# Recommender tower on one core: products reordered among the gram units, small steps moved between engines, four features of the last tile fetched by SyncE

## The chip, the cores and the metric

The kernel runs on one core of a Trainium2 chip. The core has five engines that run side by side: TensorE (PE, with its weight loads shown apart as PEld), VectorE (DVE), ScalarE (ACT), GpSimd (POOL) and SyncE (SP). They wait for one another through semaphores. The metric is device time in microseconds; smaller is better.

## The reference

A batch of 2048 rows has 27 ids each. Every id picks a row of 128 numbers from its own table. All products of two of the 27 picked rows (351 pairs) are formed, and a first layer works on the picked rows, the pairs and 16 further numbers.

```
e = stack([tbl_f[ids[:, f]] for f in range(27)], axis=1)          # 2048 x 27 x 128
inter = einsum('bfd,bgd->bfg', e, e)[:, TRIU_I, TRIU_J]           # 2048 x 351
h = concatenate([e.reshape(2048, -1), inter, dense_ctx], axis=1)  # 2048 x 3823
h = maximum(h @ W_top1 + b_top1, 0)                               # 512
h = maximum(h @ W_top2 + b_top2, 0)                               # 256
y = h @ W_top3                                                    # 2048 x 1
```

## The kernel before

The batch is cut into 16 tiles of 128 rows. Features stand in seven groups: six of four, and one of three (group 6).

GpSimd fetches a feature of a tile with one indirect DMA (L242), 128 rows into `emb`, which has a single buffer: the gathers of a group for the next tile wait until TensorE has transposed that group of this one (`s_pe_t`). TensorE transposes each feature (L269) into `ps_t`, two banks used in turn. ScalarE rounds the transposed group into the high part of `emb_x` (L534), and VectorE subtracts to get the low part (L645, counted by `s_emb_lo`). Then the group's products with the first layer's weights can run: three matmuls for each feature (L298, L299, L300, the function `multiply`), which sum into `ps_acc`.

The pair products of a tile come from 16 gram units (`gram_unit`, two matmuls each, L323) into three PSUM banks used in turn. Even units are copied out by ScalarE (L582), odd ones by VectorE (L666), four copies each (`take_blocks`); a unit waits until the bank of three units earlier is empty. Between units stand products of the same tile, as the list `BEFORE_UNIT` says: 2 ahead of unit 0, 2 of unit 3, and 1 each of units 6, 9 and 12. After units 8 and 14 the first two groups of the next tile are transposed. Behind the last unit come layer 2 of the tile before (L400) and the products not yet done, two of them in tiles 1 to 14.

In the next tile VectorE turns the copied blocks (`turn_blocks`, one stream transpose, L680), adds the two parts (L687), copies the 16 context numbers (L698) and packs the 351 pairs (L702) into `cols`. TensorE transposes `cols` (`turn_columns`, L352), ScalarE copies them out (L550, L551), and TensorE adds their products (`multiply_columns`, L356) to the tile's sum. ScalarE applies the relu (L565), TensorE transposes h1 (`turn_h1`, L393), ScalarE copies it (L571), layer 2 follows behind the gram units, and VectorE does layer 3 (L714, L717) one tile later still. The transposed columns, the transposed h1 and the result of layer 2 share one PSUM bank, `ps_late`.

The order on each engine is written out by hand. On VectorE a tile runs: split group 0, turn blocks, split 1, add parts, context, half of the pairs, split 2, the other pairs, layer 3, splits 3 to 6, then the takes of units 1, 3 to 15. The last tile has an order of its own: gram units in pairs over more banks, a separate last feature, and the pairs divided between VectorE and GpSimd. SyncE loads weights and constants at the start and then only waits to store the output.

Of the kernel before, what the change touches and what calls it, by code (L numbers as in the profile page):

```python
# [5 lines left out]
def dlrm_tower_kernel(nc, dense_ctx, ids, tables, w_top1, b_top1, w_top2, b_top2, w_top3, out):  # L6
# [6 lines left out]
    P = 128  # L13
# [35 lines left out]
    PAIRS = UNITS // 2  # L49

    POOL_FROM = 16
    HALF = H1 // 2

    ctx = ExitStack()
    with ctx:
# [15 lines left out]

        emb_x = sb("emb_x", [P, 2, P, Q], fp32r)
        emb = sb("emb", [P, NF * D])
        g_buf = sb("g_buf", [P, 2 * Q * XW])
        gram = sb("gram", [P, NF, NF])
        cols = sb("cols", [P, NCOL])
# [30 lines left out]
        s_w_late = sem("s_w_late")  # L107
        s_gather = [sem(f"s_gather{g}") for g in range(NG)]
        s_gather_last = sem("s_gather_last")
        s_zero = sem("s_zero")  # L110
        s_ident = sem("s_ident")
        s_pads = sem("s_pads")
# [11 lines left out]
        s_sum = sem("s_sum")  # L124
        s_sum_pool = sem("s_sum_pool")
        s_cols = sem("s_cols")
        s_cols_pool = sem("s_cols_pool")
        s_cols_t = sem("s_cols_t")
        s_cols_out = sem("s_cols_out")
# [6 lines left out]
        s_h2 = sem("s_h2")  # L136
        s_y = sem("s_y")
        s_stored = sem("s_stored")

        def emb_part(part, f):  # L140
            return emb_x[:, part, :, f]
# [39 lines left out]
        @block.sync  # L181
        def _(sp):
            def load_weights(c):
                s = c % STAGES
                if c >= STAGES:
                    sp.wait_ge(s_w_lo, c - STAGES + 1)
                sp.dma_start(stage[:, s, :], w_top1[c * P:(c + 1) * P, :]).then_inc(s_w_raw[s], 16)

            sp.dma_start(idx_first[:, :], ids.rearrange("(p t) f -> p t f", t=TILES)[:, 0, :]
                         ).then_inc(s_ids_first, 16)
            sp.wait_ge(s_ids_first, 16)
            for c in range(NF):
# [13 lines left out]
            sp.dma_start(w_2[:, :, :], w_top2.rearrange("(k p) n -> p k n", p=P)  # L208
                         ).then_inc(s_w_late, 16)

            rows = dense_ctx.rearrange("(q j t) c -> j q (t c)", j=NJ, t=TILES)
            for j in range(NJ):
                sp.dma_start(ctx_rows[j * Q:(j + 1) * Q, :, :].rearrange("p t c -> p (t c)"),
                             rows[j, :, :]).then_inc(s_ctx, 16)
            sp.dma_start(b2_rows[:, :], b_top2.partition_broadcast(P)).then_inc(s_const, 16)
            sp.dma_start(w3_rows[:, :],
                         w_top3.rearrange("k o -> (k o)").partition_broadcast(P)
                         ).then_inc(s_const, 16)
            sp.wait_ge(s_y, TILES)
            sp.dma_start(out.rearrange("(p t) o -> p (t o)", t=TILES),  # L220
                         y[:, :]).then_inc(s_stored, 16)
            sp.wait_ge(s_stored, 16)

        @block.gpsimd
        def _(pool):
# [5 lines left out]
            for t in range(TILES):  # L231
                if t == 1:
                    pool.wait_ge(s_ids, 16)
                for g in range(NG):
                    if t > 0:
                        pool.wait_ge(s_pe_t, NG * (t - 1) + g + 1)
                    for f in GROUPS[g]:
                        landed = s_gather[g]
# [23 lines left out]
        def _(pe):  # L262
            def turn_group(t, g):
                n = NG * t + g
                pe.wait_ge(s_gather[g], (t + 1) * 16 * len(GROUPS[g]))
                if n >= 2:
                    pe.wait_ge(s_emb_lo, n - 1)
                for i, f in enumerate(GROUPS[g]):
                    last = pe.transpose(turned_bank(n, g)[:, :, i], emb[:, f * D:(f + 1) * D],  # L269
                                        ident[:, :])  # L270
                last.then_inc(s_pe_t, 1)

            def turn_last_group(t):

                g, n = NG - 1, NG * t + NG - 1
                pe.wait_ge(s_gather[g], 16 * ((t + 1) * len(GROUPS[g]) - 1))
                pe.wait_ge(s_emb_lo, n - 1)
                for i, f in enumerate(GROUPS[g][:-1]):
                    last = pe.transpose(turned_bank(n, g)[:, :, i], emb[:, f * D:(f + 1) * D],
                                        ident[:, :])  # L280
                last.then_inc(s_pe_t, 1)

# [75 lines left out]

            def turn_columns(t):
                pe.wait_ge(s_cols, t + 1)  # L360
                if t > 0:
                    pe.wait_ge(s_h2, t)
                if t == 0:
                    pe.wait_ge(s_ones, 2)
                for n in range(NCC):
# [74 lines left out]

            BEFORE_UNIT = [2, 0, 0, 2, 0, 0, 1, 0, 0, 1, 0, 0, 1, 0, 0, 0]
            assert len(BEFORE_UNIT) == UNITS and sum(BEFORE_UNIT) <= NF - 4 * GF

            pe.wait_ge(s_ident, 1)
# [2 lines left out]
            for t in range(TILES - 1):  # L449
# [5 lines left out]
                if t > 0:  # L455
                    turn_columns(t - 1)
                turn_group(t, 4)
                if t > 0:
                    multiply_columns(t - 1)
                multiply_group(t, 3)  # L460
                turn_group(t, 5)
                if t > 0:
                    turn_h1(t - 1)
                f = 4 * GF
                for _ in range(GF if t == 0 else 2):
                    multiply(t, f)
                    f += 1
                turn_group(t, 6)
                for k in range(UNITS):
                    for _ in range(min(BEFORE_UNIT[k], NF - f)):  # L470
# [51 lines left out]
        def _(act):  # L522
# [14 lines left out]
            def split_last_group(t):  # L537
# [5 lines left out]
                act.activation(emb_part(0, NF - 1), last_feature_bank(),  # L543
                               ACT.Copy).then_inc(s_emb_hi, 1)

            def take_columns(t):
                act.wait_ge(s_cols_t, t + 1)
                if t > 0:
# [57 lines left out]
            for t in range(TILES - 1):  # L606
                for g in range(NG):
                    if t == 0:
                        for c in GROUPS[g]:
                            split_weights(c)  # L610
                    split_group(t, g)
                    if t > 0 and g == 3:
                        take_columns(t - 1)
                    if t > 0 and g == 4:
                        relu_h1(t - 1)
                    if t > 0 and g == 5:
                        take_h1(t - 1)
                for k in range(0, UNITS, 2):
                    take_blocks(t, k)
            t = TILES - 1  # L620
            for g in range(5):
                split_group(t, g)
            take_columns(t - 1)
            relu_h1(t - 1)
            split_group(t, 5)
# [9 lines left out]
        def _(dve):  # L635
# [54 lines left out]
            def pack_pairs(t, f_from, f_to):  # L690
                if f_from == 0:
                    dve.wait_ge(s_sum, t + 1)
                    if t == 0:
                        dve.wait_ge(s_ctx, 16 * NJ)
                    else:
                        dve.wait_ge(s_cols_t, t)
                    if t < TILES - 1:
                        dve.tensor_copy(cols[:, NPAIR:NPAIR + NCTX], ctx_rows[:, t, :])  # L698
                for f in range(f_from, f_to):

                    c = f * (NF - 1) - f * (f - 1) // 2
# [6 lines left out]
            def layer_3(t):  # L708
                if t == 0:
# [1 line left out]
                dve.wait_ge(s_l2, t + 1)  # L711

                result = ps_acc[:, t % 2, 0:H2] if t == TILES - 2 else ps_late[:, 0:H2]
                dve.tensor_tensor(h2[:, :], result, b2_rows[:, :],  # L714
                                  ALU.add).then_inc(s_h2, 1)
                dve.wait_ge(s_h2, t + 1)
                dve.scalar_tensor_tensor(out=h2[:, :], in0=h2[:, :], scalar=0.0,  # L717
                                         in1=w3_rows[:, :], op0=ALU.max, op1=ALU.mult,
                                         accum_out=y[:, t:t + 1]).then_inc(s_y, 1)

# [14 lines left out]
            for t in range(TILES - 1):  # L735
                for g in range(NG):
                    if t == 0:
                        for c in GROUPS[g]:
                            split_weights(c)
                    split_group(t, g)  # L740
                    if t > 0:
                        if g == 0:
                            turn_blocks(t - 1)
# [3 lines left out]
                        if g == 2:  # L747
                            pack_pairs(t - 1, 10, NF - 1)
                            if t > 1:
                                layer_3(t - 2)  # L750
                for k in range(1, UNITS, 2):
                    take_blocks(t, k)
            t = TILES - 1
            split_group(t, 0)
            split_group(t, 1)
            turn_blocks(t - 1)
            split_group(t, 2)
# [41 lines left out]
```

## Time and profile before

| | |
|---|---|
| median of 3 runs | 578.25 us (576.67 to 578.84) |
| profiled execution | span 708.0 us; the page gives no other time for it |
| TensorE busy (matmuls / weight loads) | 574.9 us (81%) / 504.6 us (71%) |
| GpSimd busy | 416.2 us (59%) |
| VectorE / ScalarE busy | 347.6 us (49%) / 232.3 us (33%) |
| mean granted TensorE clock | 0.908 of full speed |
| moved by DMA | 37.84 MB, 53 GB/s over the span |

Busy times come from the profiled execution, which took 130 us longer than the timed ones. A share of the span is a mean over stages; what sets the end has to be read from the waits and from the order of work in a tile.

### The profile page before, as it was taken

To read this page: it belongs to the slowest core of one execution; us is meant where nothing else is said; L and a number is where in the kernel's file an instruction comes from. 1 tells how busy PE (TensorE), PEld (TensorE's weight loads), DVE (VectorE), ACT (ScalarE), POOL (GpSimd) and SP (SyncE) were. 2 spreads that over 40 slices of the span, in tenths; PEclk is the share of its full clock that TensorE was granted. 3 is DMA by queue.
4 is the path that set the end of the run, shared out by engine and by line. 5 is a ranking of instruction groups with operands and counts; after the bars stand their busy time and mean duration, and the time that the engine had idled before them with its cause. 6 is when DMAs were issued, how large, how long until landed. Compare 5 with 4: busy or idle time off the path is not lost.

```text
span 708.0 us, 7882 instructions
## 1 busy us (share of the span) xinstructions
PE 574.9 (81%) x2578; PEld 504.6 (71%) x2578; DVE 347.6 (49%) x1140; ACT 232.3 (33%) x703; POOL 416.2 (59%) x450
## 2 busy tenths in 40 slices
PE   2606688989889898959959896897968979698898
PEld 1505577868778787948848795786857868697786
DVE  4305462819264563808337281554707355372755
ACT  4204423324251513315232331514315161323441
POOL 6775565666666565665746667365664666556001
PEclk9956899989989998989989899799987999989999
DMA  6613411111111111111111111011110111111000
GB/s 211 217 52 110 131 45 44 46 46 44 45 45 50 41 49 41 48 45 39 47 29 50 44 42 52 27 49 42 46 52 26 49 41 49 42 41 46 12 1 1
DMA packets 19581, 37.84 MB, mean 53 GB/s; under 512 B 7780, under 2 KB 8804, under 8 KB 19540
## 3 DMA queue, kind: packets, MB, share of 16 engines
q0 software_dynamic: 13824, 28.34, 15.1%
q1 hardware_dynamic: 5716, 8.99, 4.0%
q8 instruction: 21, 0.34, 0.2%
q14 instruction: 20, 0.16, 0.1%
HBM read 37.30 MB, written 0.01 MB: 53 GB/s over the span
## 4 chain that ended last, share of the span: by engine, by line
PE 59%; another core or an unknown queue 20%; DVE 8%; issue 6%; ACT 5%; DMA 1%; SPq 0%; ACTq 0%; DVEq 0%
PE ps_acc L298 12%; PE ps_acc L299 11%; PE ps_acc L300 11%; PE ps_gram L323 10%; DVE g_buf L666 6%; PE ps_acc L356 6%; PE ps_t L269 5%; PE ps_gram L400 3%; ACT g_buf L582 2%; DVE emb_x L645 1%; DMA g_buf<-in_W_top 1%; ACT emb_x L534 1%; ACT h_t L571 1%; PE ps_gram L352 1%
## 5 line engine op out<-in xcount | busy, mean ns | idle before, releaser
L242 POOL DMA_INDIRECT emb<-in_tbl,idx x405 | 385.8, 953 | 233.4 <-issue 109.4
L298 PE MATMUL ps_acc<-w_hi,emb_x 128*128 128x512 f32 x432 | 211.1, 489 | 28.7 <-DVE emb_x L645 26.6
L645 DVE TENSOR_TENSOR emb_x<-ps_t,emb_x 128x512 fp32r<-128x512 f32 (+1 forms) x111 | 73.9, 667 | 249.6 <-ACT emb_x L534 165.2
L299 PE MATMUL ps_acc<-w_lo,emb_x 128*128 128x512 f32 x432 | 182.7, 423 | 0.0
L300 PE MATMUL ps_acc<-w_hi,emb_x 128*128 128x512 f32 x432 | 181.0, 419 | 0.0
L666 DVE COPY g_buf<-ps_gram 32x112 f32<-32x112 f32 x480 | 129.8, 270 | 93.6 <-PE ps_gram L323 63.1
L323 PE MATMUL ps_gram<-emb_x 128*128 128x224 f32 x480 | 99.5, 335 | 79.2 <-DVE emb_x L645 41.2
L298 PEld LDWEIGHTS ps_acc<-w_hi,emb_x 128*128 128x128 f32 x432 | 131.9, 305 | 35.3 <-DVE emb_x L645 28.0
L323 PEld LDWEIGHTS ps_gram<-emb_x 128*128 128x128 f32 x480 | 83.4, 231 | 102.0 <-DVE emb_x L645 45.1
L582 ACT ACTIVATE g_buf<-ps_gram 32x112 f32<-32x112 f32 x480 | 122.2, 255 | 99.0 <-PE ps_gram L323 64.8
L534 ACT ACTIVATE emb_x<-ps_t 128x512 fp32r<-128x512 f32 (+1 forms) x111 | 63.1, 583 | 272.7 <-PE ps_t L269 137.4
L299 PEld LDWEIGHTS ps_acc<-w_lo,emb_x 128*128 128x128 f32 x432 | 134.4, 311 | 3.9
L300 PEld LDWEIGHTS ps_acc<-w_hi,emb_x 128*128 128x128 f32 x432 | 132.6, 307 | 4.2
L269 PE MATMUL ps_t<-ident,emb 128*128 128x128 f32 x429 | 68.7, 284 | 17.5 <-DMA emb<-in_tbl,idx_first 17.1
L269 PEld LDWEIGHTS ps_t<-ident,emb 128*128 128x128 f32 x429 | 53.8, 146 | 24.6 <-issue 13.2
L680 DVE STREAM_TRANSPOSE g_buf<-g_buf 128x1792 f32<-128x1792 f32 x16 | 59.2, 3697 | 0.1
L356 PE MATMUL ps_acc<-w_cols,cols_t 128*128 128x512 f32 (+1 forms) x96 | 45.5, 609 | 4.7 <-issue 3.8
L702 DVE TENSOR_TENSOR cols<-gram,g_buf 128x26 f32<-128x26 f32 (+25 forms) x406 | 39.0, 174 | 0.0
L356 PEld LDWEIGHTS ps_acc<-w_cols,cols_t 128*128 128x128 f32 (+1 forms) x96 | 17.0, 190 | 23.3 <-issue 20.8
L242 POOL DMA_INDIRECT emb<-in_tbl,idx_first x27 | 26.9, 996 | 9.2 <-issue 7.9
L400 PE MATMUL ps_gram<-w,h_t 128*128 128x256 f32 x112 | 27.0, 385 | 0.0
L400 PEld LDWEIGHTS ps_gram<-w,h_t 128*128 128x128 f32 x112 | 20.7, 195 | 2.3
(61 smaller groups left out, 163.2 us busy)
## 6 DMA issues: line engine op xcount, KB each, us to landing
g_buf<-in_W_top SPq DMA_DIRECT2D x27, 256.0 KB
emb<-in_tbl,idx POOLq DMA_INDIRECT x405
w_cols<-in_W_top SPq DMA_DIRECT2D x1, 512.0 KB
w<-in_W_top SPq DMA_DIRECT2D x1, 512.0 KB
emb<-in_tbl,idx_first POOLq DMA_INDIRECT x27
w_cols<-in_W_top SPq DMA_DIRECT2D x1, 222.0 KB
idx<-in_ids SPq DMA_DIRECT2D x1, 216.0 KB, 4.9
ctx_rows<-in_dense_ctx SPq DMA_DIRECT2D x4, 32.0 KB
```

The costliest lines, as they stand in the source:

```text
L242: pool.indirect_dma_start(out=emb[:, f * D:(f + 1) * D], out_offset=None, in_=tables[f], in_offset=bass.IndirectOffsetOnAxis(ap=rows, axis ...
L269: last = pe.transpose(turned_bank(n, g)[:, :, i], emb[:, f * D:(f + 1) * D], ident[:, :])
L298: pe.matmul(acc, emb_part(0, f), w_hi[:, f, :], start=(f == 0), stop=False)
L299: pe.matmul(acc, emb_part(0, f), w_lo[:, f, :], start=False, stop=False)
L300: last = pe.matmul(acc, emb_part(1, f), w_hi[:, f, :], start=False, stop=False)
L323: last = pe.matmul(ps_gram[:, n % BANKS, i * NJ * XW:(i + 1) * NJ * XW], gram_weights(q), gram_stream(q), start=True, stop=True)
L356: return pe.matmul(ps_acc[:, t % 2, :], cols_t[0:k, n * P:(n + 1) * P], w_cols[0:k, n, :], start=False, stop=(n == NCC - 1))
L400: last = pe.matmul(ps_late[:, 0:H2], h1_t[:, k * P:(k + 1) * P], w_2[:, k, :], start=(k == 0), stop=(k == K2 - 1))
L534: act.activation(group_part(0, g), turned_bank(n, g), ACT.Copy).then_inc(s_emb_hi, 1)
L582: last = act.activation(target, source, ACT.Copy)
L645: dve.tensor_tensor(group_part(1, g), turned_bank(n, g), group_part(0, g).bitcast(fp32), ALU.subtract).then_inc(s_emb_lo, 1)
L666: last = dve.tensor_copy(target, source)
```

## The change

Seven edits are made together.

- TensorE: the list of products among the gram units holds two ahead of units 6 and 12 instead of one, so none is left behind layer 2 in tiles 1 to 14. The products of group 3 stand ahead of the column products instead of behind them. The transposes of h1 stand two products later.
- VectorE: the low part of group 0 of the next tile is made ahead of the take of unit 15 instead of behind it.
- ScalarE copies the context numbers instead of VectorE (except in the last tile), ahead of its split of group 2; it takes the columns ahead of its split of group 4, does the relu ahead of split 5, and takes h1 behind split 6.
- VectorE leaves the first sum of layer 3 in PSUM; the next columns wait for the end of layer 3 (`s_y`) instead of that sum (`s_h2`).
- SyncE fetches features 19 to 22 of the last tile, one row at a time: for each of 128 partitions it loads four ids into registers with one load and issues four DMAs of one table row, into a buffer of their own, `ahead`. GpSimd leaves these four gathers out. TensorE waits for all 128 rows of each.

```
-            BEFORE_UNIT = [2, 0, 0, 2, 0, 0, 1, 0, 0, 1, 0, 0, 1, 0, 0, 0]
+            BEFORE_UNIT = [2, 0, 0, 2, 0, 0, 2, 0, 0, 1, 0, 0, 2, 0, 0, 0]
...
                 turn_group(t, 4)
+                multiply_group(t, 3)
                 if t > 0:
                     multiply_columns(t - 1)
-                multiply_group(t, 3)
                 turn_group(t, 5)
-                if t > 0:
-                    turn_h1(t - 1)
                 f = 4 * GF
                 for _ in range(GF if t == 0 else 2):
                     multiply(t, f)
                     f += 1
+                if t > 0:
+                    turn_h1(t - 1)
                 turn_group(t, 6)
...
             def turn_columns(t):
                 pe.wait_ge(s_cols, t + 1)
+                pe.wait_ge(s_cols_ctx, t + 1)
                 if t > 0:
-                    pe.wait_ge(s_h2, t)
+                    pe.wait_ge(s_y, t)
...
+            sp.wait_ge(s_ids, 16)
+            for p in range(P):
+                _, picked = nc.values_load_multi_w_load_instructions(
+                    idx[p:p + 1, TILES - 1, AHEAD[0]:AHEAD[-1] + 1],
+                    engines=[mybir.EngineType.SP], min_val=0, max_val=tables[AHEAD[0]].shape[0] - 1,
+                    skip_runtime_bounds_check_because="an id is a row of its table")
+                for i, f in enumerate(AHEAD):
+                    sp.dma_start(ahead[p:p + 1, i, :], tables[f][bass.ds(picked[i], 1), :]
+                                 ).then_inc(s_ahead[i], 16)
...
                     for f in GROUPS[g]:
+                        if t == TILES - 1 and f in AHEAD:
+                            continue
...
+            def place_context(t):
+                if t == 0:
+                    act.wait_ge(s_ctx, 16 * NJ)
+                else:
+                    act.wait_ge(s_cols_t, t)
+                act.activation(cols[:, NPAIR:NPAIR + NCTX], ctx_rows[:, t, :],
+                               ACT.Copy).then_inc(s_cols_ctx, 1)
...
+                    if t > 0 and g == 2:
+                        place_context(t - 1)
+                    if t > 0 and g == 4:
+                        take_columns(t - 1)
+                    if t > 0 and g == 5:
+                        relu_h1(t - 1)
                     split_group(t, g)
-                    if t > 0 and g == 3:
-                        take_columns(t - 1)
-                    if t > 0 and g == 4:
-                        relu_h1(t - 1)
-                    if t > 0 and g == 5:
+                    if t > 0 and g == 6:
                         take_h1(t - 1)
...
-                if t < TILES - 1:
-                    dve.tensor_copy(cols[:, NPAIR:NPAIR + NCTX], ctx_rows[:, t, :])
...
-                dve.tensor_tensor(h2[:, :], result, b2_rows[:, :],
-                                  ALU.add).then_inc(s_h2, 1)
+                dve.tensor_tensor(result, result, b2_rows[:, :], ALU.add).then_inc(s_h2, 1)
...
-                    split_group(t, g)
+                    if t == 0 or g > 0:
+                        split_group(t, g)
...
                 for k in range(1, UNITS, 2):
+                    if k == UNITS - 1:
+                        split_group(t + 1, 0)
                     take_blocks(t, k)
             t = TILES - 1
-            split_group(t, 0)
             split_group(t, 1)
             turn_blocks(t - 1)
```

## Rows read from the trace of the kernel before

**Rows 1.** page, its first line and the shares of the chain by engine.

```profile
span 708.0 us, 7882 instructions
...
PE 59%; another core or an unknown queue 20%; DVE 8%; issue 6%; ACT 5%; DMA 1%; SPq 0%; ACTq 0%; DVEq 0%
```

**Rows 2.** waits, whole span: engine, line, waited for, total us, times, longest.

```profile
ACT emb_x L534 <- remote: 106.9, 16, 27.5
POOL emb L242 <- PE ps_t L269: 94.0, 35, 9.3
```

**Rows 3.** timeline of GpSimd: start us, us, engine, line, op, count [idle before, releaser].

```profile
2.78 1.14 POOL L242 DMA_INDIRECT emb<-in_tbl,idx_first  x1 [1.30 <-DMA idx_first<-in_ids]
...
36.65 0.94 POOL L242 DMA_INDIRECT emb<-in_tbl,idx_first  x1 [0.30 <-issue]
...
655.83 0.94 POOL L242 DMA_INDIRECT emb<-in_tbl,idx  x1 [0.30 <-issue]
```

**Rows 4.** timeline of TensorE, tile 2 to tile 3.

```profile
166.69 0.30 PEld L323 LDWEIGHTS ps_gram<-emb_x 128*128 128x128 f32 x2
...
166.92 1.60 PEld L400 LDWEIGHTS ps_gram<-w,h_t 128*128 128x128 f32 x8
...
168.54 0.30 PEld L298 LDWEIGHTS ps_acc<-w_hi,emb_x 128*128 128x128 f32 x1
...
169.96 0.30 PEld L298 LDWEIGHTS ps_acc<-w_hi,emb_x 128*128 128x128 f32 x1
...
172.84 0.58 PEld L269 LDWEIGHTS ps_t<-ident,emb 128*128 128x128 f32 x4
...
173.41 0.59 PE L298 MATMUL ps_acc<-w_hi,emb_x 128*128 128x512 f32 x1
...
180.99 0.30 PEld L356 LDWEIGHTS ps_acc<-w_cols,cols_t 128*128 128x128 f32 x2 [0.44 <-issue]
```

**Rows 5.** timeline of ScalarE, the same boundary.

```profile
165.52 2.13 ACT L582 ACTIVATE g_buf<-ps_gram 32x112 f32<-32x112 f32 x8 [0.21 <-issue]
...
167.67 1.08 ACT L534 ACTIVATE emb_x<-ps_t 128x512 fp32r<-128x512 f32 x2
```

**Rows 6.** timeline of VectorE, the same boundary.

```profile
162.56 5.78 DVE L666 COPY g_buf<-ps_gram 32x112 f32<-32x112 f32 x20 [1.16 <-PE ps_gram L323]
...
168.37 0.69 DVE L645 TENSOR_TENSOR emb_x<-ps_t,emb_x 128x512 fp32r<-128x512 f32 x1
...
168.98 3.71 DVE L680 STREAM_TRANSPOSE g_buf<-g_buf 128x1792 f32<-128x1792 f32 x1
...
172.60 0.66 DVE L645 TENSOR_TENSOR emb_x<-ps_t,emb_x 128x512 fp32r<-128x512 f32 x1
...
175.26 0.67 DVE L645 TENSOR_TENSOR emb_x<-ps_t,emb_x 128x512 fp32r<-128x512 f32 x1
```

**Rows 7.** timeline of TensorE, two waits among gram units of tile 6.

```profile
324.04 0.48 PE L323 MATMUL ps_gram<-emb_x 128*128 128x224 f32 x2 [0.44 <-DVE g_buf L666]
...
328.36 0.49 PE L323 MATMUL ps_gram<-emb_x 128*128 128x224 f32 x2 [0.45 <-DVE g_buf L666]
```

**Rows 8.** timeline of TensorE, tile 0 to tile 1.

```profile
90.50 0.61 PE L298 MATMUL ps_acc<-w_hi,emb_x 128*128 128x512 f32 x1 [1.94 <-issue]
...
92.59 0.63 PE L299 MATMUL ps_acc<-w_lo,emb_x 128*128 128x512 f32 x1
93.02 0.63 PE L300 MATMUL ps_acc<-w_hi,emb_x 128*128 128x512 f32 x1
```

**Rows 9.** windows: stretch, us, busy us (count) by engine, granted clock, DMA.

```profile
92.10:95.40 3.30, 3.30 (x11) 2.62 (x11) 3.28 (x3) 0.00 (x0) 0.94 (x1) 0.50 0.16 40
```

**Rows 10.** timeline of TensorE in the last tile.

```profile
663.46 1.89 PE L400 MATMUL ps_gram<-w,h_t 128*128 128x256 f32 x8
...
683.69 0.27 PE L286 MATMUL ps_t<-ident,emb 128*128 128x128 f32 x1
```

**Rows 11.** timeline of SyncE at the start.

```profile
2.52 1.75 SPq L187 DMA_DIRECT2D g_buf<-in_W_top  x4
```

More of the change, by code:

```diff
@@ L51, in dlrm_tower_kernel @@
     POOL_FROM = 16
+    AHEAD = list(range(19, 23))
+    assert (NF * (TILES - 1) + AHEAD[0]) % 4 == 0
     HALF = H1 // 2
@@ L73, in dlrm_tower_kernel @@
         emb = sb("emb", [P, NF * D])
+        ahead = sb("ahead", [P, len(AHEAD), D])
         g_buf = sb("g_buf", [P, 2 * Q * XW])
@@ L109, in dlrm_tower_kernel @@
         s_gather_last = sem("s_gather_last")
+        s_ahead = [sem(f"s_ahead{f}") for f in AHEAD]
         s_zero = sem("s_zero")
@@ L126, in dlrm_tower_kernel @@
         s_cols = sem("s_cols")
+        s_cols_ctx = sem("s_cols_ctx")
         s_cols_pool = sem("s_cols_pool")
@@ L138, in dlrm_tower_kernel, with rows_of, gathered @@
         s_stored = sem("s_stored")
+        def rows_of(t, f):
+            if t == TILES - 1 and f in AHEAD:
+                return ahead[:, f - AHEAD[0], :]
+            return emb[:, f * D:(f + 1) * D]
+        def gathered(t, g):
+            last = len([f for f in GROUPS[g] if f in AHEAD]) if t == TILES - 1 else 0
+            return 16 * ((t + 1) * len(GROUPS[g]) - last)
         def emb_part(part, f):
@@ L237, in _ @@
                     for f in GROUPS[g]:
+                        if t == TILES - 1 and f in AHEAD:
+                            continue
                         landed = s_gather[g]
@@ L264, in turn_group @@
                 n = NG * t + g
-                pe.wait_ge(s_gather[g], (t + 1) * 16 * len(GROUPS[g]))
+                pe.wait_ge(s_gather[g], gathered(t, g))
+                if t == TILES - 1:
+                    for f in GROUPS[g]:
+                        if f in AHEAD:
+                            pe.wait_ge(s_ahead[f - AHEAD[0]], 16 * P)
                 if n >= 2:
@@ L268, in turn_group @@
                 for i, f in enumerate(GROUPS[g]):
-                    last = pe.transpose(turned_bank(n, g)[:, :, i], emb[:, f * D:(f + 1) * D],
+                    last = pe.transpose(turned_bank(n, g)[:, :, i], rows_of(t, f),
                                         ident[:, :])
@@ L278, in turn_last_group @@
                 for i, f in enumerate(GROUPS[g][:-1]):
-                    last = pe.transpose(turned_bank(n, g)[:, :, i], emb[:, f * D:(f + 1) * D],
+                    last = pe.transpose(turned_bank(n, g)[:, :, i], rows_of(t, f),
                                         ident[:, :])
@@ L622, in _ @@
                 split_group(t, g)
+                if g == 1:
+                    place_context(t - 1)
             take_columns(t - 1)
@@ L692, in pack_pairs @@
                     dve.wait_ge(s_sum, t + 1)
-                    if t == 0:
-                        dve.wait_ge(s_ctx, 16 * NJ)
-                    else:
+                    if t > 0:
                         dve.wait_ge(s_cols_t, t)
-                    if t < TILES - 1:
-                        dve.tensor_copy(cols[:, NPAIR:NPAIR + NCTX], ctx_rows[:, t, :])
                 for f in range(f_from, f_to):
@@ L713, in layer_3 @@
                 result = ps_acc[:, t % 2, 0:H2] if t == TILES - 2 else ps_late[:, 0:H2]
-                dve.tensor_tensor(h2[:, :], result, b2_rows[:, :],
-                                  ALU.add).then_inc(s_h2, 1)
+                dve.tensor_tensor(result, result, b2_rows[:, :], ALU.add).then_inc(s_h2, 1)
                 dve.wait_ge(s_h2, t + 1)
-                dve.scalar_tensor_tensor(out=h2[:, :], in0=h2[:, :], scalar=0.0,
+                dve.scalar_tensor_tensor(out=h2[:, :], in0=result, scalar=0.0,
                                          in1=w3_rows[:, :], op0=ALU.max, op1=ALU.mult,
```

## The prediction

> **What bounds the kernel now.** I read the page first. Its span is 708.0 us, 130 us above the median of 578.25 us, and it puts 20% of the chain, some 141 us, down to a releaser that it can't name [rows 1]. The page gives no time for what lies around the span, so the sum below is a difference, worked out from parts of the trace in which no such wait stands, and then set on the median. The waits say where the 130 us sit: ScalarE's split of the turned features waited 106.9 us in 16 stretches for something without a name, and the gathers waited 94.0 us for TensorE's transposes [rows 2]. About one such wait falls in each tile. I take them to belong to the profiled execution alone, since 708 less 141 is 567, close to what runs without a profile need.
>
> Two things can set the pace without them. GpSimd issues one gather every 1.25 us (0.94 busy, 0.30 between) [rows 3], so 27 gathers take 33.7 us a tile and all 432 take 540 us. With the first at 2.8 us, some 3.5 us from the last issue to its turned feature (an estimate) and 24.3 us from that transpose, at 683.7 us, to the end of the span [rows 10], the gathers alone ask for about 570 us. The other is TensorE's written order. If tile 0's last feature is turned at about 40 us (its gather starts at 36.65, [rows 3]), fifteen periods and 24.3 us must fit into 578.25: a period is at most (578.25 - 40 - 24.3) / 15 = 34.3 us. So TensorE's loop and the gathers are within 0.6 us a tile of each other, and whatever lengthens TensorE's loop by more than that shows in the time.
>
> Then I read one tile boundary engine by engine, from gram unit 15 of one tile to the second group of products of the next. Unit 15's weights load at 166.69, layer 2 runs from 166.92, two left-over products from 168.54, group 0 from 169.96, its twelve matmuls 0.24 us apart, the transposes of group 2 from 172.84, and group 1 starts at 173.41 with no wait [rows 4]. ScalarE finishes its last two block takes at 167.65 and goes straight into the splits of groups 0 and 1, which take 1.08 us together [rows 5], about 0.6 for one with its end. VectorE has finished take 15 at 168.34, subtracts group 0 at 168.37, transposes the blocks from 168.98 and subtracts group 1 at 172.60, done at 173.26 [rows 6]. TensorE asks for group 1 at 173.4. That is a tie of 0.15 us, and nearly all boundaries of this kind show it.
>
> **The change, part by part.** *Split of group 0 ahead of take 15, and two products moved from behind layer 2 into the gram units.* These go together. VectorE can't begin the split before ScalarE has ended its own: 167.67 + 0.6 = 168.27 [rows 5]. Before, VectorE used that time for take 15, from about 167.2. After, it waits about 1.1 us, splits until 168.98, copies block 15 in 1.16 us (twenty copies, five takes, in 5.78), transposes until 173.8 and has group 1 ready at about 174.4 [rows 6]. TensorE no longer has 1.44 us of products (169.96 - 168.54, [rows 4]) behind layer 2. It waits some 0.5 us for group 0, starts it at 169.05, is through with it and the transposes 3.45 us later (173.41 - 169.96) at 172.5, and then waits about 2 us for group 1. From unit 15 to group 1 the way grows by 1.1 us. Everything behind it keeps its order: group 2 was ready at 175.93 [rows 6], and would be at about 176.9 against TensorE's wish at 177.9.
>
> The 1.44 us come back in the gram region. There two units of a tile waited 0.44 and 0.45 us for VectorE's copies [rows 7], with one product ahead of their triple. A second product in each place fills these waits. Bounds: if the waits are filled altogether, the region grows by 1.44 - 0.89 = 0.55 us; if the copies before them, which the added product also lets catch up, give another 0.3, by 0.25. With no filling it is 1.44. I take 0.3, nearer to the rows.
>
> *Products of group 3 ahead of the columns, first-layer transposes two products later.* The column matmuls waited 0.44 us before their first weights [rows 4]; of that some 0.2 us is the switch between forms that stays. Gain 0.2 us. Between column matmuls and the transposes of h1 stand a group of transposes and two products, 1.9 us, against a relu of 0.6, so no wait replaces it.
>
> *Context copy to ScalarE, layer 3 in PSUM.* VectorE loses a copy of 0.17 us in the stretch behind group 1, where it is now early by a microsecond again: nothing. ScalarE gets it ahead of the split of group 2, whose transposes it waits for anyway. The sum in PSUM was read from PSUM before too; I cost it at nothing between -0.05 and +0.1 us. The columns now wait for the end of layer 3 rather than its first half, 0.45 us later, with 1.6 us of room: nothing.
>
> *SyncE's 512 fetches.* They take four gathers, 5.0 us, from GpSimd's last tile. But from layer 2 at 663.46 to the last transpose at 683.69 TensorE works without a wait [rows 10], with all gathers issued by 656.8 [rows 3]. TensorE needs nearly the whole period for this tile, so if the gathers set the pace the gain is what TensorE has in hand, 0 to 0.6 us, not 5. Queued behind the fetches on SyncE is only the output. Price of a partition's turn: four issues at 0.44 us [rows 11] is 1.75 us as the lower bound; the register load and address work have no row. There is room for 128 turns of about 4 us each, from about 47 us (tile 0's transposes done, constants issued) to some 32 us before the end. I take it as hidden. The Trainium skill, DMA: Bandwidth & Descriptors, section on latency and other measured facts, gives a register load from a tensor a floor of about 600 ns; by it a turn is an estimated 2.4 us, 301 us in all, hidden as well, which no row here shows.
>
> **The sum.** Per full tile 1.1 + 0.3 - 0.2 = +1.2 us, fourteen times: +16.8 us. The last tile's boundary has its group 1 split ahead of the transpose and adds nothing but the 0.3. If the gathers held TensorE back before, part of this is absorbed: between 0 and 0.6 us a tile, I take 0.25, -3.5 us.
>
> The clock adds to it. At the boundary of tile 0, where layer 2 doesn't stand, TensorE idled for 1.94 us ahead of group 0, and the granted clock was then 0.50 (1.2 GHz of 2.4) from 92.1 to 95.4 us [rows 8, 9]. Matmuls were then 0.43 us apart rather than 0.24 [rows 4, 8], which costs 3.4 x (1 - 0.24 / 0.43) = 1.5 us. The new wait of about 2.1 us is of that kind and comes in each tile. Bounds: no fall, 0; one in every tile, 14 x 1.5 = 21 us. Of the idle stretches above 1.6 us in the trace most were followed by a fall, but many of them stand beside the nameless waits and may have been longer than recorded. I take half: +10.5 us. Together 16.8 - 3.5 + 10.5 = +23.8, which is 602.0 us on the median, and about 732 on the profiled span if the nameless waits stay as they are.
>
> **The rivals.** *The wait without the clock.* The same 1.2 us a tile, but 2.1 us of idling amid dense work leave the clock at 1.0. For it: the two levels depend on more than one idle stretch, and this one is shorter than the 3 us before most of the falls. 578.25 + 16.8 - 3.5 = 591.5 us.
>
> *Hidden behind the gathers.* TensorE's real loop is below 32.5 us, because its records are stretched by the profile; the gathers set the pace before and after, and the wait fits into the room. The last tile gives back 1 us or so. 577 to 579 us. Against it: matmuls 0.24 us apart and column matmuls at 0.43 add up to nearly 34 us with what stands between.
>
> *Faster.* VectorE's way from unit 15 to group 1 is the place. If without the profile it is 30% shorter than the recorded 7.6 us, TensorE never waits for it, and the filled 0.9 us and the column gap of 0.2 come off each tile, until the gathers stop it at 33.7 us: 15 x (34.2 - 33.7) = 7 us, 571 us. The point from which it decides is 5.4 us for that way. Against it: VectorE's parts repeat to a few hundredths of a microsecond in all tiles.
>
> *SyncE comes late.* A turn above 4.1 us makes the last tile wait at its group 4; each 0.1 us more costs 12.8 us. At 4.5 us the end is 47 + 576 + 32 = 655 us.
>
> **How the numbers follow.** Forecast with clock falls 0.44; wait without them 0.28; hidden 0.14; faster 0.10; SyncE late 0.04. A difference under 0.5%, 2.9 us, can't be told from none. Slower 0.76, same 0.14, faster 0.10. The range takes in the first three cases: from 577 (hidden) to 616 (a fall in every tile, nothing absorbed, 578 + 16.8 + 21). The forecast's own range is 594 to 616.
>
> **What would show it.** In the profile of the changed kernel: VectorE idle for about 1.1 us ahead of the split of group 0, its stream transpose 1.1 us later after unit 15; the first matmul of group 1 waiting some 2 us for VectorE, in each of fourteen tiles; no waits of gram units 8 and 14; no gap ahead of the column matmuls; the granted clock at 0.50 behind the new wait. I am wrong if group 1 starts without a wait, if SyncE's last fetch lands after the last tile's third group, or if GpSimd has no wait for TensorE's transposes left.

## The result, and the profile after

The changed kernel takes 606.8 us (605.96 to 608.17, 4 runs) against 577.94 us; the ratio is 1.0512, 95% interval 1.0492 to 1.0531. It is 28.9 us slower, where +23.8 had been forecast.

The page of the changed kernel, its span and its chain by engine; they answer to [rows 1]:

```profile
span 604.2 us, 9544 instructions
...
PE 67%; DVE 16%; ACT 6%; POOL 5%; issue 4%; DMA 1%; ACTq 0%; DVEq 0%; POOLq 0%
```

The releaser without a name is gone from the chain, and the span is 1.8 us below that execution's own time of 605.96 us. VectorE, 8% of the chain of [rows 1], now has 16%.

The waits of the changed kernel (engine, line waited for: total us, times, longest):

```profile
PE ps_acc L330 <- DVE emb_x L690: 29.5, 28, 2.1
...
POOL emb L270 <- PE ps_t L301: 12.8, 16, 2.3
```

TensorE waits 29.5 us for VectorE's low part of the split, where the trace of before has such waits at its start alone. The boundary from tile 3 to tile 4, all engines, answers to [rows 4 to 6]:

```profile
160.39 0.48 PE L355 MATMUL ps_gram<-emb_x 128*128 128x224 f32 x2 [0.25 <-ACT g_buf L623]
...
160.71 1.90 PE L433 MATMUL ps_gram<-w,h_t 128*128 128x256 f32 x8
...
161.44 1.08 ACT L567 ACTIVATE emb_x<-ps_t 128x512 fp32r<-128x512 f32 x2
162.07 0.69 DVE L690 TENSOR_TENSOR emb_x<-ps_t,emb_x 128x512 fp32r<-128x512 f32 x1 [1.44 <-ACT emb_x L567]
...
162.68 1.11 DVE L711 COPY g_buf<-ps_gram 32x112 f32<-32x112 f32 x4
...
162.91 0.58 PE L330 MATMUL ps_acc<-w_hi,emb_x 128*128 128x512 f32 x1 [0.30 <-DVE emb_x L690]
...
163.89 3.62 DVE L725 STREAM_TRANSPOSE g_buf<-g_buf 128x1792 f32<-128x1792 f32 x1
...
165.89 0.60 PE L301 MATMUL ps_t<-ident,emb 128*128 128x128 f32 x4
...
167.55 0.69 DVE L690 TENSOR_TENSOR emb_x<-ps_t,emb_x 128x512 fp32r<-128x512 f32 x1
...
168.29 0.62 PE L330 MATMUL ps_acc<-w_hi,emb_x 128*128 128x512 f32 x1 [1.81 <-DVE emb_x L690]
```

Read it from gram unit 15 (160.39) on. ScalarE splits groups 0 and 1 at 161.44. VectorE has stood idle for 1.44 us (1.1 forecast) when it subtracts group 0 at 162.07. Only then comes take 15 (162.68), then the block transpose (163.89), then group 1 (167.55 to 168.24). TensorE starts group 0 at 162.91, is through with the transposes of group 2 at about 166.5 and waits until 168.29: 1.81 us. From unit 15 to group 1 it is 7.90 us here, where [rows 4] has 173.41 less 166.69, 6.7 us.

Windows of the changed kernel at this boundary, and at the one before it, tile 2 to tile 3 (stretch, length, busy us and count by engine, granted clock, share and rate of DMA):

```profile
165.60:169.10 3.50, 1.69 (x9) 1.38 (x9) 3.44 (x3) 0.60 (x1) 2.58 (x4) 1.00 0.20 52
169.10:172.50 3.40, 3.40 (x10) 2.68 (x9) 3.37 (x29) 0.00 (x0) 2.67 (x3) 0.50 0.19 49
...
127.10:133.10 6.00, 3.95 (x18) 3.47 (x17) 5.82 (x8) 0.80 (x3) 4.64 (x5) 1.00 0.21 56
133.10:136.60 3.50, 3.50 (x17) 3.42 (x18) 3.46 (x26) 0.00 (x0) 2.72 (x3) 1.00 0.18 48
```

After the wait at 166.5 the granted clock is 0.50, the 1.2 GHz level, for 3.4 us. At the earlier boundary TensorE waited from 131.23 to 132.98, as long, and the clock stayed at 1.00. There are thirteen such waits, twelve of 1.75 to 1.81 us and one of 2.13, at the boundaries from tile 1 on; seven were followed by a fall. The tiles show the two cases apart: from unit 15 to the next tile's it is 35.32 us without a fall and 36.83 with one.

### The profile page after: what moved, and what is told of

It reads as the page before. It is cut to its first block, busy times and chain, and to the rows that moved or that the text cites. A ratio compares the mean times of both kernels' runs of the same rounds, so it can differ in the third digit from the quotient of the medians.

```text
span 604.2 us, 9544 instructions
## 1 busy us (share of the span) xinstructions
PE 545.0 (90%) x2578; PEld 484.1 (80%) x2578; DVE 347.4 (57%) x1125; ACT 232.2 (38%) x718; POOL 414.1 (69%) x446
## 4 chain that ended last, share of the span: by engine, by line
PE 67%; DVE 16%; ACT 6%; POOL 5%; issue 4%; DMA 1%; ACTq 0%; DVEq 0%; POOLq 0%
PE ps_acc L330 17%; PE ps_acc L332 14%; PE ps_acc L331 14%; DVE g_buf L725 9%; PE ps_gram L355 8%; PE ps_acc L388 7%; POOL emb L270 5%; PE ps_t L301 5%; ACT g_buf L623 4%; DVE emb_x L690 4%; DVE g_buf L711 3%; ACT emb_x L567 2%; PE ps_gram L426 1%; DMA emb<-in_tbl,idx 1%; PE ps_gram L384 1%
## 5 line engine op out<-in xcount | busy, mean ns | idle before, releaser
L330 PE MATMUL ps_acc<-w_hi,emb_x 128*128 128x512 f32 x432 | 204.3, 473 | 29.5 <-DVE emb_x L690 29.5
L332 PE MATMUL ps_acc<-w_hi,emb_x 128*128 128x512 f32 x432 | 177.5, 411 | 0.0
L331 PE MATMUL ps_acc<-w_lo,emb_x 128*128 128x512 f32 x432 | 177.3, 411 | 0.0
L301 PE MATMUL ps_t<-ident,emb 128*128 128x128 f32 x425 | 67.2, 280 | 21.6 <-DMA emb<-in_tbl,idx_first 19.8
L355 PEld LDWEIGHTS ps_gram<-emb_x 128*128 128x128 f32 x480 | 69.2, 189 | 14.0 <-ACT g_buf L623 6.8
L301 PEld LDWEIGHTS ps_t<-ident,emb 128*128 128x128 f32 x425 | 52.2, 145 | 34.7 <-issue 21.7
L355 PE MATMUL ps_gram<-emb_x 128*128 128x224 f32 x480 | 75.5, 285 | 4.7 <-ACT g_buf L623 3.5
L388 PE MATMUL ps_acc<-w_cols,cols_t 128*128 128x512 f32 (+1 forms) x96 | 44.0, 593 | 0.1
L606 ACT ACTIVATE h<-ps_acc 128x512 f32<-128x512 f32 x15 | 9.0, 598 | 72.2 <-PE ps_acc L388 72.2
L270 POOL DMA_INDIRECT emb<-in_tbl,idx_first x27 | 28.2, 1045 | 9.2 <-issue 7.6
```

Source lines behind the costliest of these rows:

```text
L270: pool.indirect_dma_start(out=emb[:, f * D:(f + 1) * D], out_offset=None, in_=tables[f], in_offset=bass.IndirectOffsetOnAxis(ap=rows, axis ...
L301: last = pe.transpose(turned_bank(n, g)[:, :, i], rows_of(t, f), ident[:, :])
L330: pe.matmul(acc, emb_part(0, f), w_hi[:, f, :], start=(f == 0), stop=False)
L331: pe.matmul(acc, emb_part(0, f), w_lo[:, f, :], start=False, stop=False)
L332: last = pe.matmul(acc, emb_part(1, f), w_hi[:, f, :], start=False, stop=False)
L355: last = pe.matmul(ps_gram[:, n % BANKS, i * NJ * XW:(i + 1) * NJ * XW], gram_weights(q), gram_stream(q), start=True, stop=True)
```

## The experiments

All times below are medians; the kernel before, run beside them, had 576.7 to 577.0 us.

**The kernel before once more.** The profile of before had 130 us more than its timed runs, and nothing in the prediction could compare tile by tile.

> The kernel before, unchanged, profiled once more. If the 130 us above the timed median, and the waits without a name, belonged to that one profiled execution, the span is now about 575 us, group 1 starts about 6.3 us after gram unit 15, and a tile takes about 34.0 us. If they belong to the kernel, the span is about 700 us again.

It ran in 577.71 us, in one run. Its span and its busy shares, then its gathers' wait for TensorE, then the boundary from tile 3 to tile 4:

```profile
span 575.9 us, 7882 instructions
## 1 busy us (share of the span) xinstructions
PE 534.1 (93%) x2578; PEld 479.4 (83%) x2578; DVE 347.4 (60%) x1140; ACT 232.1 (40%) x703; POOL 416.4 (72%) x450
```

```profile
POOL emb L242 <- PE ps_t L269: 3.4, 11, 0.3
```

```profile
157.07 0.49 PE L323 MATMUL ps_gram<-emb_x 128*128 128x224 f32 x2 [0.45 <-DVE g_buf L666]
...
157.75 0.46 PE L323 MATMUL ps_gram<-emb_x 128*128 128x224 f32 x2
...
158.67 1.08 ACT L534 ACTIVATE emb_x<-ps_t 128x512 fp32r<-128x512 f32 x2
...
159.40 0.69 DVE L645 TENSOR_TENSOR emb_x<-ps_t,emb_x 128x512 fp32r<-128x512 f32 x1
...
160.01 3.70 DVE L680 STREAM_TRANSPOSE g_buf<-g_buf 128x1792 f32<-128x1792 f32 x1
...
163.64 0.65 DVE L645 TENSOR_TENSOR emb_x<-ps_t,emb_x 128x512 fp32r<-128x512 f32 x1
...
164.44 0.59 PE L298 MATMUL ps_acc<-w_hi,emb_x 128*128 128x512 f32 x1
```

The 130 us belonged to that one profiled execution. Here the granted clock is at 1.0 in every full tile, TensorE is busy for 93% of the span, GpSimd waits 3.4 us for transposes instead of the 94.0 of [rows 2], and each of the thirteen periods from tile 1's unit 15 to tile 14's is 33.93 us. Group 1 starts at 164.44 with no wait, 0.15 us after VectorE has it ready. From the start of unit 15 to unit 15's copy, splits, block transpose and group 1, each offset is that of [rows 4 to 6] within 0.05 us: the disturbed trace had the boundary right. Cut at the same three points, a tile is (the middle of unit 15 is the end of the first of its two matmuls):

| from ... to | before | changed | difference | forecast |
|---|---|---|---|---|
| middle of unit 15 to group 1 | 6.34 | 7.53 | +1.19 | +1.1 |
| group 1 to unit 0 | 17.30 | 16.98 | -0.32 | -0.2 |
| unit 0 to middle of unit 15 | 10.30 | 10.81 | +0.51 | +0.3 |
| a tile | 33.93 | 35.32 | +1.39 | +1.2 |
| a fall of the clock, when there is one | none | +1.51 | +1.51 | +1.5 |

Thirteen periods at +1.39 and seven falls at 1.51 make 28.6 us; the spans differ by 28.3.

**Take 15 first again.** In the changed kernel:

```
                 for k in range(1, UNITS, 2):
-                    if k == UNITS - 1:
-                        split_group(t + 1, 0)
                     take_blocks(t, k)
+                    if k == UNITS - 1:
+                        split_group(t + 1, 0)
```

> The changed kernel with take 15 ahead of the split of group 0 again; the list of products stays. My theory (VectorE's way from unit 15 to group 1 holds TensorE): the split doesn't start earlier or later, since ScalarE's half ends at 1.3 us after unit 15 either way, so group 0 starts at 2.1 us as in the changed kernel, but group 1 comes 1.2 us earlier, a tile takes 34.1 us, and the clock doesn't fall since the wait shrinks from 1.8 to 0.6 us: 606.8 - 14 x 1.2 - 7 x 1.5 = 579 us. Rival (the moved products are what costs, since nothing stands behind layer 2): it stays above 595 us.

Measured 576.88 us, ratio to before 1.0002 (0.9984 to 1.0019). TensorE at the boundary from tile 3 to tile 4:

```profile
159.00 0.58 PE L330 MATMUL ps_acc<-w_hi,emb_x 128*128 128x512 f32 x1 [0.30 <-DVE emb_x L690]
...
161.98 0.60 PE L301 MATMUL ps_t<-ident,emb 128*128 128x128 f32 x4
163.02 0.62 PE L330 MATMUL ps_acc<-w_hi,emb_x 128*128 128x512 f32 x1 [0.44 <-DVE emb_x L690]
```

Group 0 starts as late as in the changed kernel, for want of ScalarE, and has the same 0.30 us of idling ahead of it. Group 1 waits 0.44 us instead of 1.81. A tile is 33.96 us, the clock falls nowhere from tile 2 to tile 14, and these two lines alone give back all 30 us. 579 had been expected.

**The wait filled.** Six matmuls of no use stand in the wait; their result is not used.

```
                 turn_group(t, 2)
+                if t > 0:
+                    pe.wait_ge(s_act_raw, UNITS // 2 * t)
+                    pe.wait_ge(s_dve_raw, UNITS // 2 * t)
+                    for _ in range(6):
+                        pe.matmul(ps_gram[:, 0, :], emb_part(0, 0), w_hi[:, 0, :],
+                                  start=True, stop=True)
                 multiply_group(t, 1)
```

> The changed kernel with six products of no use (features of group 0 into an emptied gram bank, result unused) ahead of group 1 of tiles 1 to 14, 1.44 us into a wait of 1.8. It tells the clock's share from the wait's. My theory: VectorE's way is untouched, the seven falls of the clock go, 7 x 1.5 = 10.5 us: 596 us, every tile 35.3 us. Rival (TensorE's work counts, the wait is not what bounds): the added 14 x 1.44 = 20 us show, 627 us. If falls have another cause: 607 us.

Measured 597.39 us, ratio 1.0363 (1.0326 to 1.0401). TensorE at the same boundary; the six are the middle row:

```profile
163.06 0.58 PE L330 MATMUL ps_acc<-w_hi,emb_x 128*128 128x512 f32 x1 [0.30 <-DVE emb_x L696]
...
166.40 1.74 PE L489 MATMUL ps_gram<-w_hi,emb_x 128*128 128x512 f32 x6
168.49 0.62 PE L330 MATMUL ps_acc<-w_hi,emb_x 128*128 128x512 f32 x1 [0.36 <-DVE emb_x L696]
```

84 matmuls more, and 9.4 us less. Group 1 comes 7.6 us after the middle of unit 15, as in the changed kernel, tiles take 35.3 to 35.4 us (one 35.7), and from tile 2 on no full tile has the clock below 1.0. So 20 us of the loss stay when the clock doesn't fall, and 10 are the clock behind the wait.

**The two costly edits alone, on the kernel before.**

```
-            BEFORE_UNIT = [2, 0, 0, 2, 0, 0, 1, 0, 0, 1, 0, 0, 1, 0, 0, 0]
+            BEFORE_UNIT = [2, 0, 0, 2, 0, 0, 2, 0, 0, 1, 0, 0, 2, 0, 0, 0]
...
-                    split_group(t, g)
+                    if t == 0 or g > 0:
+                        split_group(t, g)
...
                 for k in range(1, UNITS, 2):
+                    if k == UNITS - 1:
+                        split_group(t + 1, 0)
                     take_blocks(t, k)
             t = TILES - 1
-            split_group(t, 0)
```

> The kernel before with two edits alone: two products moved from behind layer 2 into the gram units, and the split of group 0 ahead of take 15. My theory: these two are the whole loss; without the gap of 0.2 us that the other edits close it is 607 + 3 = 610 us. Rival (the other edits, SyncE's fetches or the context copy carry part of the loss): below 600 us.

Measured 613.8 us, ratio 1.0635 (1.0593 to 1.0676): more than the 610 expected. A tile is 35.69 us without a fall and 37.16 with one. The 0.37 us a tile above the changed kernel are what the other edits save, nearly all of it between group 1 and unit 0 (17.33 us against 16.98); I had counted 0.2. In the profiled execution, of 617.97 us, the clock fell behind eleven of the thirteen waits instead of seven: 13 x 0.37 + 4 x 1.5 = 10.8 us, against 12.0 between the two profiled executions. Its mean granted clock was 0.956, and 0.967 to 0.972 in the other runs of this kernel, which were 3 to 5 us shorter, so the number of falls seems to vary from run to run. What decides which of these waits is followed by a fall is left open: waits of the same length, 1.75 to 1.8 us, stand on both sides.

**The early split with the old list.** The changed kernel with the list of before: two products behind layer 2.

```
-            BEFORE_UNIT = [2, 0, 0, 2, 0, 0, 2, 0, 0, 1, 0, 0, 2, 0, 0, 0]
+            BEFORE_UNIT = [2, 0, 0, 2, 0, 0, 1, 0, 0, 1, 0, 0, 1, 0, 0, 0]
```

> The changed kernel with the old list of products: two stand behind layer 2 again, and the split of group 0 stays ahead of take 15. It parts the two edits. My theory: group 1 still comes 7.53 us after unit 15, since VectorE's way sets it, but TensorE reaches it later and waits 1.1 us instead of 1.8, and the gram region is 0.5 us shorter: 34.8 us a tile, 14 x 0.5 = 7 us less than the changed kernel without falls, 589 us if the shorter wait leaves the clock alone, up to 600 us if it falls as often as before. Rival (it needs both edits for a loss): 577 us.

Measured 588.48 us, ratio 1.0190 (1.0160 to 1.0221). TensorE at the boundary from tile 3 to tile 4:

```profile
165.56 0.60 PE L301 MATMUL ps_t<-ident,emb 128*128 128x128 f32 x4
167.08 0.61 PE L330 MATMUL ps_acc<-w_hi,emb_x 128*128 128x512 f32 x1 [0.93 <-DVE emb_x L690]
```

Group 1 is at 7.5 us again, and a tile is 34.79 us. The wait is 0.93 us (1.25 in one tile), and no fall followed from tile 2 to tile 14. The early split thus puts group 1 at 7.5 us whatever the list is; the moved products cost 0.51 us of gram region and turn a wait that leaves the clock alone into one that in about half of the tiles doesn't.

**The other edits alone.** The list and the order of take 15 as before; order around the columns, context copy, layer 3 in PSUM and fetches as in the changed kernel.

> The changed kernel without its two costly edits: the old list of products among the units, take 15 ahead of the split. Left are the order around the columns, the context copy, layer 3 in PSUM and SyncE's fetches. My theory: from group 1 to unit 0 the way is 0.32 us shorter, as in the changed kernel, so a tile asks for 33.6 us against 33.93 before; the gathers ask for 33.7. Gain 14 x 0.25 = 3.5 us, 573 to 574 us. Rival (the gathers held the kernel before, and the fetches take 5 us from them): below 572 us. Rival (the fetches disturb): 577 us or more.

Measured 576.98 us over twelve runs from 573.96 to 579.98, ratio 1.0002 (0.9979 to 1.0025). The gain of 3.5 us didn't come. In the profile, whose span is 573.2 us, nine periods are 33.6 us as expected (33.96 with the moved products, in the run with take 15 first: there they eat what the columns' order saves), and the last four 34.1 to 34.65. There TensorE's transposes wait for gathers:

```profile
447.58 0.55 PE L301 MATMUL ps_t<-ident,emb 128*128 128x128 f32 x3 [0.16 <-DMA emb<-in_tbl,idx]
...
473.48 0.66 PE L301 MATMUL ps_t<-ident,emb 128*128 128x128 f32 x4 [0.42 <-DMA emb<-in_tbl,idx]
```

The four combinations of the two costly edits, the others in place, now stand side by side, as a tile's time without a fall of the clock: neither 33.59 us, the list alone 33.96 (take 15 first), the early split alone 34.79 (the old list), both 35.32. The split costs 1.20 us with the old list and 1.36 with the new; the list 0.37 without the split and 0.53 with it.

GpSimd needs 33.72 us for a tile at its steady 1.25 us a gather, but in a tile now and then a gather or two takes longer (34.1 to 34.7 us in eight of fourteen tiles here). TensorE's loop at 33.59 is below that. The timed runs scatter over 6 us, which fits gathers that are late to a varying degree; that they are the cause in the timed runs too is inferred.

**SyncE's fetches.** First the changed kernel without them: features 19 to 22 of the last tile go through GpSimd as all others.

```
-    AHEAD = list(range(19, 23))
+    AHEAD = []
...
-            for p in range(P):
-                _, picked = nc.values_load_multi_w_load_instructions(...)
-                for i, f in enumerate(AHEAD):
-                    sp.dma_start(ahead[p:p + 1, i, :], ...).then_inc(s_ahead[i], 16)
```

> The changed kernel without SyncE's fetches: GpSimd gathers all features again. My theory: with 35.3 to 36.8 us a tile against 33.7 for the gathers these are hidden, and nothing changes: 607 us, within 1. Rival (GpSimd's last tile counted): 612 us. Rival (512 small fetches had slowed something): 604 us or less.

Measured 608.04 us, ratio 1.0543 (1.0515 to 1.0572) beside the changed kernel's 1.0512: intervals that overlap, no difference shown. Its profiled execution has eight falls of the clock instead of seven, and its tiles the same 35.3 and 36.8 us. Then the fetches as the only edit on the kernel before (the loop above added, GpSimd's four gathers taken out).

> The kernel before with SyncE's fetches as its only edit. My theory: TensorE sets the pace at 33.93 us a tile, the gathers ask for 33.7, so four gathers less in the last tile give 0 to 1 us: 576 to 577 us. Rival (the gathers held the kernel before): 572 us.

Measured 576.81 us, ratio 0.9991 (0.9976 to 1.0006): nothing. SyncE in the changed kernel, all 512 fetches:

```profile
47.23 294.09 SPq L243 DMA_DIRECT2D ahead<-in_tbl  x512
```

They run from 47.2 to 341.3 us, 2.30 us for a partition's four, and are there some 230 us before the last tile's group 4 is transposed at 571.9.

**A version without the wait.** The take comes first again, and VectorE subtracts group 1 ahead of the block transpose, not behind it.

```
-                    if t == 0 or g > 0:
+                    if t == 0 or g > 1:
                         split_group(t, g)
                     if t > 0:
                         if g == 0:
+                            split_group(t, 1)
                             turn_blocks(t - 1)
...
                 for k in range(1, UNITS, 2):
+                    take_blocks(t, k)
                     if k == UNITS - 1:
                         split_group(t + 1, 0)
-                    take_blocks(t, k)
```

> The changed kernel with take 15 ahead of the split, and on VectorE the split of group 1 ahead of the block transpose, as the last tile has it. My theory: group 1 is ready 2.7 us after unit 15 and TensorE reaches it at 5.6 without a wait; a tile asks for 10.8 + 5.6 + 17.0 = 33.4 us. The gathers' 33.7 are nearly the bound: 569 us, up to 571. Rival (VectorE is then late for group 2, wanted 9.0 us after unit 15, at 8.9 to 9.0): a new wait there of 0.3 us or more, 573 us or more.

Measured 573.11 us, ratio 0.9929 (0.9911 to 0.9947): 0.7% below the kernel before, and 2 to 4 us above the 569 to 571 expected. The boundary from tile 3 to tile 4, VectorE and TensorE:

```profile
158.40 1.29 DVE L690 TENSOR_TENSOR emb_x<-ps_t,emb_x 128x512 fp32r<-128x512 f32 x2
...
159.24 0.58 PE L330 MATMUL ps_acc<-w_hi,emb_x 128*128 128x512 f32 x1 [0.30 <-DVE emb_x L690]
...
159.60 3.71 DVE L725 STREAM_TRANSPOSE g_buf<-g_buf 128x1792 f32<-128x1792 f32 x1
...
162.28 0.60 PE L301 MATMUL ps_t<-ident,emb 128*128 128x128 f32 x4
...
162.64 0.59 PE L330 MATMUL ps_acc<-w_hi,emb_x 128*128 128x512 f32 x1
```

VectorE subtracts both groups in one go at 158.40, and the transposes of group 2 run straight into group 1 (162.64). TensorE's loop falls to 33.39 us, and from tile 6 on it is held at 33.5 to 33.8: the gathers' pace. The rival's number, 573, came without its cause: from tile 2 to tile 14 TensorE never waits for group 2's low part, and the waits that are new, 0.1 to 0.2 us at a time, are for gathers. Without the fetches:

> The kernel of the run before without SyncE's fetches. Once TensorE's tile is below 33.7 us the gathers set the pace: the last one can't be issued before 541 us, which with 3.2 us to its transpose, 24.3 us behind it and 2 us around the span gives 571 us. With the fetches that floor is 5 us lower. My theory: 571 us, 2 us above the run with fetches. Rival (TensorE still sets the pace): no difference.

Measured 575.32 us, ratio 0.9970 (0.9952 to 0.9987), 4 us more than expected: in the profiled execution (576.94 us) GpSimd issued its last gather at 548.4 us and not at 541, since six single gathers of tiles 1 to 5 were late by 0.3 to 0.5 us and one of the last tile, at 537.9, by 1.8. TensorE in the last tile:

```profile
542.18 0.66 PE L291 MATMUL ps_t<-ident,emb 128*128 128x128 f32 x4 [1.69 <-DMA emb<-in_tbl,idx]
...
550.97 0.33 PE L308 MATMUL ps_t<-ident,emb 128*128 128x128 f32 x1 [0.85 <-DMA emb<-in_tbl,idx]
```

Once TensorE no longer sets the pace, the last tile's transposes stand and wait 1.69 and 0.85 us for gathers (part of it is that one late gather), and over the timed runs the fetches are worth 2.2 us; 2 had been expected. If so, the lead should be of more use a few tiles earlier:

```
+    AT = 11
...
-            if t == TILES - 1 and f in AHEAD:
+            if t == AT and f in AHEAD:
...
-            last = len([f for f in GROUPS[g] if f in AHEAD]) if t == TILES - 1 else 0
+            last = len([f for f in GROUPS[g] if f in AHEAD]) if t >= AT else 0
...
-                    idx[p:p + 1, TILES - 1, AHEAD[0]:AHEAD[-1] + 1],
+                    idx[p:p + 1, AT, AHEAD[0]:AHEAD[-1] + 1],
```

> The version with the split of group 1 ahead of the block transpose, with SyncE's four features taken from tile 11 (they are there by about 341 us, and wanted at about 404) instead of from tile 15. My theory: the gathers hold tiles 6 to 14 at 33.75 us there against TensorE's 33.39; a lead of 5 us from tile 11 on lets four tiles run at 33.39 and costs nothing at the end: 1 to 1.5 us less, about 572 us. Rival (only the last tile's gathers count): 575 us, as without fetches.

Measured 571.21 us, ratio 0.9892 (0.9867 to 0.9917): 5.7 us below before, the lowest of all, though its interval just overlaps that of the same fetches for tile 15 (0.9911 to 0.9947). The periods that end in tiles 7 to 10 are 33.6 to 33.8 us, and those after them 33.4 to 33.5 again.

## Why the prediction was right, point by point

**The tie on VectorE's way was the whole matter.** The prediction's step from the early split to a wait of about 2 us for group 1 holds: 1.8 us at each of thirteen boundaries (at the fourteenth, from tile 0, it is 0.65), the way longer by 1.19 us against 1.1. Undoing the one reordering on VectorE removed the loss altogether. The other signs named ahead came too: the block transpose starts 3.50 us after unit 15 instead of 2.29, units 8 and 14 don't wait, the column products follow the last product 0.24 us later (179.74 and 179.98) with no gap, and GpSimd still waits 12.8 us for transposes.

**Gram region.** The term was too small, +0.51 against +0.3 and within the bounds of 0.25 to 1.44. The two waits of [rows 7] are indeed gone. A new one of 0.25 us stands ahead of unit 15 (160.39 in the boundary above), for ScalarE's take of unit 12. The plain filling of the two waits, 0.55 us, would have served better than the extra 0.3 credited for copies that catch up, but it too comes near by luck: 0.90 us of waits went and 0.25 came, and without its waits the region is 1.17 us longer, not the 1.44 of two products.

**Column gap.** -0.32 us against -0.2: more of the 0.44 us went away than assumed.

**Absorption.** This step was wrong. I had let the gathers hold TensorE back by up to 0.6 us a tile and took 0.25, -3.5 us. The clean profile has a period of 33.93 us with no wait for a gather in a full tile, above the gathers' 33.7. TensorE's order set the pace, nothing was absorbed. Of the 5.1 us between forecast and result 3.5 are this term; 1.3 are the tile's (13 x 1.39 = 18.1 against 14 x 1.2 = 16.8).

**The clock.** Half of the waits followed by a fall was taken, at 1.5 us; seven of thirteen at 1.51 us came. The price was read from rows, the rate was a guess that came out by luck: the kernel with the two edits alone had eleven, the changed kernel without fetches eight. The rival without the clock had the same mechanism otherwise; with the wait filled the kernel took 597.4 us, against its 591.5.

**What was costed at nothing** came out so. The fetches were run by themselves; context copy and layer 3 in PSUM only together with the order around the columns: the tile's 33.59 us without the costly edits is 0.34 us below 33.93, and the column gap alone gives 0.32. For the fetches the reasons held as well: no gain while TensorE sets the pace, hidden on SyncE. The estimate of 2.4 us a turn that rested on the Trainium skill, DMA: Bandwidth & Descriptors, section on latency and other measured facts, stands beside 2.30 us measured for a turn with its load. The trace bears out both of its parts: the load takes 0.56 us (median of 128, a little below the 0.6 in the estimate), and the fetches of a turn start 0.41 to 0.45 us apart, where 0.44 had been taken.

**The nameless waits** were rightly taken for the profiled execution's own, and its 0.30, 1.25 and 0.24 us steps recur in the clean one. The 732 us forecast for the changed kernel's span held only if they stayed; they were of that execution, not of the kernel, and didn't come back (604.2 us).

The rival of the faster kernel needed VectorE's way 30% shorter without those disturbances, and it isn't. Its "recorded 7.6 us" misreads the rows: from unit 15 to group 1's low part [rows 4, 6] have 6.57 us (166.69 to 173.26), and so has the clean trace; 7.6 is that way with the takes in the new order, for which the changed kernel has 7.85 (160.39 to 168.24). SyncE came 1.8 us a turn below the 4.1 from which it would have been late.

## What to carry to other kernels

Before an item is moved ahead of another on an in-order engine, ask what that engine was doing with the time: here VectorE could not begin the split any sooner, because ScalarE's half of it ended at the same moment, so the move only pushed the take, the transpose and the next group behind an idle microsecond. Two chains that arrive together, here within 0.15 us, are both critical, and covering work must not be taken from between them. A bound just below the one that is being removed (33.7 below 33.9 us a tile) takes most of the next gain; the relief for it is worth nothing before and something after, and, in the two placements tried, more where its lead serves more tiles.

## What the runs showed of the hardware that wasn't expected

A profiled execution can be 130 us longer than the next one of the same program, 708.0 against 575.9 us of span, with waits that nothing in the trace releases; its undisturbed stretches agree with the clean one to some hundredths of a microsecond. An idle stretch of TensorE of 1.8 us amid dense matmuls was followed by 3.4 us at 1.2 GHz in seven of thirteen cases in one kernel, in eight in a second and in eleven in a third; none followed from tile 2 to tile 14 in the kernels whose longest wait there was 0.3 to 1.25 us. The timed execution is 1.8 us longer than its span. SyncE's row fetch by a register takes 0.23 us to issue, about half of the 0.43 us of a weight load in [rows 11], but with the register instructions between them the fetches follow one another every 0.41 to 0.45 us, the weight loads every 0.47.
